# Embedding tower kernel: units in phases, four fixed slots for stacked chunks, tables and weight splitting on ACT's queue

## The reference, cut to what matters

```python
e = jnp.stack([tbl_f[ids[:, f]] for f in range(39)], axis=1)      # 2048 x 39 x 32
p, q = e[:, ROW, :], e[:, COL, :]                                 # all 741 pairs i < j
z = jnp.einsum('bpc,apc,bpa->bp', p, w, q)                        # w is 32 x 741 x 32
h = jnp.concatenate([z, dense_ctx], axis=1)                       # 757 columns
h = jnp.maximum(h @ W_top1 + b_top1, 0.0)                         # 512
h = jnp.maximum(h @ W_top2 + b_top2, 0.0)                         # 256
y = h @ W_top3                                                    # 1
```

## Time and profile before

| what | value |
|---|---|
| median of 3 runs | 873.27 us |
| the profiled execution | 877.21 us |
| its span, first to last instruction | 875.4 us |
| mean granted TensorE clock | 0.932 of full speed |
| PE busy | 734.8 us (84%) |
| DVE (VectorE) busy | 655.0 us (75%) |
| POOL (GpSimd) busy | 589.1 us (67%) |
| ACT (ScalarE) busy | 92.4 us (11%) |
| moved by DMA | 149.90 MB, mean 171 GB/s |

### The profile page before, as it was taken

One profiled execution on the slowest core, in us unless ns is written; L12 is line 12 of the kernel. 1 busy time (PEld: TensorE's weight loads), 2 busy tenths in 40 slices (PEclk: granted clock), 3 DMA queues, 4 the chain that ended last, 5 costly groups with the idle time before them and its releaser, 6 DMA issues.

```text
span 875.4 us, 11491 instructions
## 1 busy us (share of the span) xinstructions
PE 734.8 (84%) x4378; PEld 291.6 (33%) x4378; DVE 655.0 (75%) x786; ACT 92.4 (11%) x153; POOL 589.1 (67%) x752
## 2 busy tenths in 40 slices
PE   2603567387998969999999699999999799999998
PEld 1201122122332424443433244444433244444333
DVE  4603759466989947899898679999999478998750
ACT  2202000110010101010101111001111010111002
POOL 6899999998169999997599999982999940000000
PEclk9856688788999989999999899999999899999999
DMA  6677663658654567633664647444734575326000
GB/s 162 207 267 271 216 199 106 224 169 288 229 171 159 157 198 227 228 123 101 228 185 154 199 145 244 136 143 164 248 107 154 189 240 172 142 70 207 22 0 1
DMA packets 71036, 149.90 MB, mean 171 GB/s; under 512 B 12782, under 2 KB 22081, under 8 KB 70853
## 3 DMA queue, kind: packets, MB, share of 16 engines
q1 hardware_dynamic: 58684, 142.83, 47.0%
q0 software_dynamic: 12288, 6.32, 5.0%
q10 hardware_dynamic: 8, 0.01, 0.0%
HBM read 115.49 MB, written 33.62 MB: 170 GB/s over the span
## 4 chain that ended last, share of the span: by engine, by line
PE 64%; DMA 14%; DVE 12%; issue 5%; SPq 4%; ACT 1%; DVEq 0%; ACTq 0%
PE z_ps L541 21%; PE u_ps L517 20%; PE t_ps L495 8%; PE m_ps L554 7%; DVE prod L773 6%; DVE one_hot L761 5%; DMA e<-scratch 5%; DMA w_rows<-h 3%; DMA scratch<-parts 3%; PE m_ps L556 2%; DMA hot_idx<-hot 2%; PE t_ps L480 1%; SPq L412 1%; PE u_ps L576 1%; PE u_ps L585 1%
## 5 line engine op out<-in xcount | busy, mean ns | idle before, releaser
L773 DVE TENSOR_TENSOR prod<-u_ps,eT 128x1024 f32<-128x1024 f32 x400 | 469.7, 1216 | 127.6 <-PE u_ps L517 126.6
L330 POOL DMA_INDIRECT e_rows<-in_tbl_dram,idx x384 | 382.3, 996 | 121.4 <-issue 65.3
L517 PE MATMUL u_ps<-e,w 128*128 128x512 f32 x800 | 263.0, 443 | 97.0 <-DMA e<-scratch 50.6
L541 PE MATMUL z_ps<-prod,sel 128*32 128x512 f32 x1600 | 268.7, 624 | 0.0
L517 PEld LDWEIGHTS u_ps<-e,w 128*128 128x128 f32 x800 | 135.6, 195 | 244.2 <-issue 114.4
L337 POOL MEMSET pause<- 128x512 f32 x364 | 207.6, 570 | 0.2
L495 PE MATMUL t_ps<-one_hot,tb 125*32 125x512 bf16 x1560 | 150.2, 399 | 28.2 <-DVE one_hot L761 27.8
L761 DVE TENSOR_SCALAR one_hot<-hot_idx,row 125x512 bf16<-125x512 f16 (+2 forms) x320 | 155.2, 539 | 20.0 <-DMA hot_idx<-hot 16.1
L495 PEld LDWEIGHTS t_ps<-one_hot,tb 125*32 125x32 bf16 x1560 | 56.3, 101 | 124.4 <-issue 82.6
L541 PEld LDWEIGHTS z_ps<-prod,sel 128*32 128x32 f32 x1600 | 44.5, 110 | 141.4 <-issue 122.6
L554 PE MATMUL m_ps<-zT,w1s 128*128 128x512 f32 x144 | 73.2, 592 | 0.0
(11 more groups left out here) (42 smaller groups left out, 101.9 us busy)
## 6 DMA issues: line engine op xcount, KB each, us to landing
w<-w_rows SPq DMA_DIRECT2D x100, 512.0 KB, 5.4
e<-scratch SPq DMA_DIRECT2D x72, 512.0 KB, 4.9
scratch<-parts SPq DMA_DIRECT2D x72, 256.0 KB, 2.2
w_rows<-h SPq DMA_DIRECT2D x24, 512.0 KB, 6.3
e_rows<-in_tbl_dram,idx POOLq DMA_INDIRECT x384
hot_idx<-hot SPq DMA_DIRECT2D x12, 512.0 KB, 6.8
h<-in_w_dram SPq DMA_DIRECT2D x6, 512.0 KB, 4.5
e<-scratch SPq DMA_DIRECT2D x8, 384.0 KB, 4.1
```

Of the source, the lines that this page charges most:

```text
L330: pool.indirect_dma_start(e_rows[:, r, n, D * q:D * q + D], None, tables[f], bass.IndirectOffsetOnAxis(ap=idx[:, t, f * TPG + n:f * TPG + ...
L517: last = nc.tensor.matmul(u_ps[:, s % 2, place, :], w4[:, p % WR, (u % PW) * P:(u % PW + 1) * P], e4[:, chunk_no(t, g) % ES, j - C * g, :] ...
L541: last = nc.tensor.matmul(z_ps[D * quad:D * quad + D, z % 2, :], sel[:, D - 1 - row:2 * D - 1 - row], prod[:, (NS * t + n) % PR, place, :] ...
L773: nc.vector.tensor_tensor(prod[:, s % PR, :, :], u_ps[:, s % 2, :, :], e, ALU.mult).then_inc(s_mul, 1)
```

## The change

The units are ordered in phases, one for each chunk, in the order 0, 1, 2, 3, 7, 8, 4, 5, 6, 9. A phase has all units in which its chunk meets a chunk that came earlier, whichever of the two is the stacked one. The sizes of the phases are 3, 7, 11, 15, 19, 23, 27, 31, 35 and 29 units, the same as those of the ten chunks before. Chunk 7 is now needed from unit 36, chunk 8 from unit 55 (batch 13, second step), and the stacked chunk 4 from unit 86. The slices of chunks 7 and 8 are taken two to a batch, in batches 1 to 10 of a tile (in the first tile 0 to 2 and 5 to 9), and those of chunks 1 and 2 of the next tile in batches 36 to 47. `e4` has four slots and a chunk has a fixed one. `w4` has four slots instead of six. The weights are split in pieces of 16 units with two rooms, and their loads and stores and the table loads are issued by ACT. Chunk 8's tables are split in batch 1. In ACT's program, a load of weights waits until the stores of the piece two before it have landed. The copies of the ids (15 instead of 4) are one for each table. The dense layers' weights are loaded in batch 12.

```diff
+HOT_TABLES = {1: ((0, 8), (1, 10), (2, 8), (3, 8)), 2: ((1, 8), (2, 8), (3, 8)), 7: ((0, 10), (1, 8), (2, 8), (3, 8)),
+              8: ((0, 10), (1, 8), (2, 10), (3, 10))}
...
-UNITS = [(j // C, gi, j) for j in range(F) for gi in range(j // C + 1) if C * gi < j]
+PHASES = (0, 1, 2, 3, 7, 8, 4, 5, 6, 9)
+
+
+def units_of_phase(n):
+    g = PHASES[n]
+    earlier = PHASES[:n]
+    against = [(y, g, C * y + q) for y in earlier if y > g for q in range(fields_in(y))]
+    own = [(g, gi, C * g + q) for q in range(fields_in(g)) for gi in sorted(x for x in earlier if x < g) + [g] if C * gi < C * g + q]
+    return against + own
+
+
+UNITS = [u for n in range(NG) for u in units_of_phase(n)]
...
-WR = 6
-ES = 3
+WR = 4
+ES = 4
+
+E4_SLOT = {0: 0, 1: 2, 2: 3, 3: 1, 7: 2, 8: 3, 4: 0, 5: 1, 6: 0, 9: 1}
...
-PREPS = {0: (2,), 3: (3,), 11: (4,), 19: (5,), 27: (6,)}
-PREP_UNITS = [(0, 8)] + [(8 + 32 * k, 40 + 32 * k) for k in range(6)]
...
+PREP_UNITS = [(16 * k, min(NU, 16 * k + 16)) for k in range(-(-NU // 16))]
+PREPS_FIRST = 3
+PREPS = {4 * (k - PREPS_FIRST): k for k in range(PREPS_FIRST, len(PREP_UNITS))}
...
+FIRST_TILE = ((7, 0, None, (0, 0, 0, 1, 1, 1, 2, 2, 2, 2)), (3, 0, 3, ()), (8, 0, None, (5, 5, 6, 6, 7, 7, 8, 8, 9, 9)),
+              (4, 0, 14, ()), (5, 0, 21, ()), (6, 0, 28, ()), (9, 0, 35, ()),
+              (1, 1, None, (36, 37, 38, 38, 39, 39, 40, 40, 41, 41)), (0, 1, 42, ()), (2, 1, 43, (43, 44, 45, 45, 46, 46, 47, 47)))
+OTHER_TILES = ((3, 0, 0, ()), (7, 0, None, (1, 1, 2, 2, 3, 3, 4, 4, 5, 5)), (8, 0, None, (6, 6, 7, 7, 8, 8, 9, 9, 10, 10)),
+               (4, 0, 14, ()), (5, 0, 20, ()), (6, 0, 27, ()), (9, 0, 35, ()),
+               (1, 1, None, (36, 37, 38, 38, 39, 39, 40, 40, 41, 41)), (0, 1, 42, ()), (2, 1, 43, (43, 44, 45, 45, 46, 46, 47, 47)))
+LAST_TABLE_BATCH = 1
```

SP's list ahead of the first batch becomes:

```diff
             sp.wait_ge(s_hot16, 32)
             load_hot_indices((0, 1))
             load_hot_indices((0, 2))
...
             bring_piece(0, 0)
+            bring_piece(0, 1)
+            load_hot_indices((0, 7))
             store_parts((0, 1))
-            stack_chunk((0, 1))
-            store_weights(1)
-            load_weights(2)
             store_parts((0, 0))
             stack_chunk((0, 0))
-            for p in range(1, 5):
-                bring_piece(0, p)
-            load_table(8)
+            stack_chunk((0, 1))
             store_parts((0, 2))
+            bring_piece(0, 2)
             stack_chunk((0, 2))
```

ACT's program gets the loads and stores:

```diff
+            def load_weights(k):
+                a, b = PREP_UNITS[k]
+                if k >= 2:
+                    act.wait_ge(s_wout[k % 2], 64 * (k // 2))
+                act.dma_start(w_in_room[k % 2][:, 0:(b - a) * D], w[:, a * P:b * P].rearrange("a (s n) -> a s n", s=C)
+                              ).then_inc(s_wraw[k % 2], 16)
...
+            def weights_rest(k):
+                a, b = PREP_UNITS[k]
+                act.wait_ge(s_wlo, k + 1)
+                for h in range(2):
+                    act.dma_start(w_rows[:, h, 1, a * P:b * P].rearrange("a (s n) -> a s n", s=C),
+                                  w_in_room[k % 2][:, 0:(b - a) * D]).then_inc(s_wout[k % 2], 16)
+                if k + 2 < len(PREP_UNITS):
+                    load_weights(k + 2)
...
+            load_table(1)
+            load_weights(0)
+            load_weights(1)
             act.wait_ge(s_idx, 16)
...
+            load_table(2)
             act.wait_ge(s_idt, 1)
...
             table_high(1)
+            weights_high(0)
             table_middle(1)
-            weights_high(0)
             table_high(2)
+            weights_rest(0)
+            load_table(7)
             table_middle(2)
+            weights_high(1)
+            table_high(7)
+            weights_rest(1)
+            table_middle(7)
             take_chunk((0, 1))
-            weights_high(1)
             take_chunk((0, 0))
-            table_high(7)
-            table_middle(7)
+            weights_high(2)
             take_chunk((0, 2))
-            table_high(8)
-            table_middle(8)
+            load_table(8)
+            weights_rest(2)
             for t in range(NT):
                 for b in range(NBAT):
                     if t == 0 and b in PREPS:
-                        for k in PREPS[b]:
-                            weights_high(k)
+                        weights_high(PREPS[b])
+                        weights_rest(PREPS[b])
+                    if t == 0 and b == LAST_TABLE_BATCH:
+                        table_high(HOT_CHUNKS[-1])
+                        table_middle(HOT_CHUNKS[-1])
```

VectorE's list ahead of the first batch:

```diff
             table_rest(1)
+            weights_low(0)
             table_low(1)
+            table_rest(2)
...
-            for k in range(slices_of(1)):
+            for k in range(OS):
                 one_hot_slice((0, 1), k)
-            weights_low(0)
-            table_rest(2)
             table_low(2)
+            weights_low(1)
+            table_rest(7)
+            for k in range(OS, slices_of(1)):
+                one_hot_slice((0, 1), k)
+            table_low(7)
             split_chunk((0, 1))
-            weights_low(1)
...
             split_chunk((0, 0))
+            weights_low(2)
...
-            table_rest(7)
-            table_low(7)
             split_chunk((0, 2))
-            table_rest(8)
-            table_low(8)
+            for c, k in TAKES.get(0, ()):
+                one_hot_slice(c, k)
```

More of the change, by code:

```diff
@@ L132, in rows_count, with e4_before, e4_loads @@
     n = GPOS[c]
-    return sum(16 * TPG * gathered(GATHERED[x][1]) for x in range(n % ER, n + 1, ER))
+    return sum(16 * TPG * len(gathered(GATHERED[x])) for x in range(n % ER, n + 1, ER))
+def e4_before(c):
+    t, g = c
+    same = [x for x in PHASES if E4_SLOT[x] == E4_SLOT[g]]
+    n = same.index(g)
+    return (t, same[n - 1]) if n else (t - 1, same[-1]) if t else None
+def e4_loads(c):
+    same = [x for x in PHASES if E4_SLOT[x] == E4_SLOT[c[1]]]
+    return len(same) * c[0] + same.index(c[1]) + 1
 TURNS, TAKES, COMPLETE, INDICES, STACKS = {}, {}, {}, {}, {}
@@ L166, in spread_mlp @@
         slices = sum(list(x[3]).count(b) for x in OTHER_TILES if not (last and x[1]))
-        work[b] = 3 * slices + (2 if any(x[2] == b for x in OTHER_TILES) else 0)
+        work[b] = 3 * slices + (3 if any(x[2] == b for x in OTHER_TILES) else 0)
     taken = []
@@ L238, in tower @@
         hroom = h1[:, :, :].rearrange("p m n -> p (m n)")
-        w_in_room = hroom[:, 0:2 * NB]
-        w_hi_room = hroom[:, 2 * NB:4 * NB].bitcast(F32R)
+        w_in_room = [hroom[:, k * NB:(k + 1) * NB] for k in range(2)]
+        w_hi_room = [hroom[:, (2 + k) * NB:(3 + k) * NB].bitcast(F32R) for k in range(2)]
         ids_f = prod[:, 0, :, :].rearrange("p u n -> p (u n)")[:, 0:NT * HOT_FIELD_COLS]
         def table_room(g):
-            first, rows = HOT_ROWS[g, 0], sum(HOT_SLICES[g][1])
+            first, rows = HOT_ROWS[g, 0], sum(HOT_SLICES[g])
             if g == HOT_CHUNKS[-1]:
@@ L326, in _ @@
                     pool.wait_ge(s_tp, GPOS[c] - ER + 1)
-                for q in range(gathered(g)):
+                for q in gathered(c):
                     f = C * g + q
@@ L595, in _ @@
             transpose_ids()
-            for g, turned, slices in BEGIN:
-                if turned:
+            for g in BEGIN:
+                if gathered((0, g)):
                     turn((0, g))
-                for k in slices:
-                    look_up((0, g), k)
+                if hot((0, g)):
+                    for k in range(slices_of(g)):
+                        look_up((0, g), k)
             pe.wait_ge(s_sel, 16)
@@ L753, in one_hot_slice @@
                 for tall in (False, True):
[L754 removed]
+                    here = [(i, x) for i, x in enumerate(fields) if (HOT_SLICES[g][x] > HK) == tall]
                     for a, (i, x) in enumerate(here):
```

171 lines of the change are left out of this document (76 added, 95 removed), and 3 rows, old and new, of the table OTHER_TILES.

## The result

The changed kernel takes 871.6 us (median of 20 runs, 866.98 to 875.05) against 874.46 us for the kernel before (20 runs, 872.66 to 878.73). The ratio is 0.9965, 95% interval 0.995 to 0.9979: faster by a third of a per cent, where 848 was forecast and 868 was the end of the range. The profiled execution took 875.05 us, the slowest of the 20; its span is 872.9 us, against 875.4.

The account below looks back on a forecast made before the run. It took the start and tile 0 (301 us, waits in queue order) and then DVE or PE by batch as bounds. 877.2 - 39 + 14 = 852, as a median 848; own range 834 to 862, 8 in 10 822 to 868.

Parts of the forecast that it names:

- The start: Before the first multiply: it comes at 59 us instead of 75.3, -16 us; 54 to 65 with other store landings.
- the price of a 256 KB store: In the start, ACT waits for weight stores to land: 4.5 us taken, between 3.2 and 6.3.
- its own first sign of being wrong: Wrong if the start is late because ACT's waits for stores are longer than 4.5 us.
- Tile 0: First tile: DVE's work of 176 us plus waits, 203 taken; it ends at 262 instead of 301.1, -23 for the tile.
- Chunk 3 was to be 7 us late: Tile 0: chunk 3, turned in batch 3 behind chunk 7's slices and wanted in batch 5, comes 7 us late.
- Tiles 1 to 3: Later tiles: 190, 190 and 181 us instead of 185.4, 183.7 and 178.6, +14 us in all.
- The wait in batch 2: Tiles 1 to 3: PE's wait for stacked chunk 2 goes, -8.6, -9.6 and -9.2 us at most.
- the wait in batch 13: Tiles 1 to 3: a new wait for stacked chunk 8, 4 us idle and 1 for the clock.
- (d): Rival: ACT is tile 0's bottleneck, standing for stores; tile 0 gains nothing, only the start does: 871 us, chance 0.08.
- (b): Rival: transfers, not waiting, bound the start; the first multiply stays near 75 us: 864 us, chance 0.14.
- (a): Rival: the new wait for chunk 8 does not come; tiles 1 to 3 at 185: 833 us, chance 0.17.
- (c): Rival: chunks 7 and 8 come late in every tile, 19 us a tile instead of 5: 899 us, chance 0.09.

Follow-up runs that it names:

- third_first: Changed kernel with the edits of late_load and early_slices, plus the first tile's chunk 3 turned in batch 0 ahead of chunk 7's slices: 833.85 us, ratio 0.9536.
- late_load: Changed kernel with ACT loading a weight piece after rounding the one before, not right behind the stores it must wait for: 854.4 us, ratio 0.9768.
- early_slices: Changed kernel with the slices of chunks 7 and 8 one batch earlier in tiles 1 to 3: 860.67 us, ratio 0.9847.
- short one-hots: Changed kernel and kernel before, one-hots of chunks 7 and 8 in tiles 1 to 3 cut to 32 columns: 858.88 and 871.87 us beside 876.31.
- queues_only: Changed kernel with the order of units, batches of turns and slices, ES = 3 and WR = 6 of before: 863.37 us, ratio 0.9873.
- four_slots: Kernel before with four slots for stacked chunks and the next tile's first chunks taken earlier: 877.29 us beside 902.24, ratio 0.9716.

## Why the prediction was wrong, step by step

**The start: wrong, and 16.9 us of the miss.** The failing step is the price of a 256 KB store: "between 3.2 and 6.3 us I take 4.5". The median is 3.6, but the one pair on which ACT stood took 15.9 from the first issue (58.0) to the landing (73.9), outside both ends; each store by itself took 8.3 and 11.6 from its own issue. The chain of the prediction gives the pair 5.5 us (51.5 to 57), so that this term alone is 10.4 us short. Both ends were medians over the whole span, while this store leaves when two stacks, a table of four DMAs and the scratch stores are all under way, and a third stack comes at 67. The prediction gave the share of the earlier trace rows as 0.78 and used it only for a rival; it should have bounded the landing by it. A second term was too small: ACT took chunks 1, 0 and 2 at 44, 46 and 55 instead of 37, 39 and 47, since DVE's last seven slices of chunk 1 took 9 us, not 6, and began 3 later. By that the stores left at 58.0 instead of 51.5, the other 6.5 us. The prediction had named the first of these as its own first sign of being wrong. With the late load the first multiply came at 59.3, but that it is the number forecast is luck: there ACT takes chunk 2 at 50, not 47, and waits for no store ahead of the first multiply.

**Tile 0: right in sum (207.6 for 203), not in its terms.** Chunk 3 was to be 7 us late; PE waited 15.1 us for it, and the batch took 12 too many:

```profile
120.84 1.65 PE L518 MATMUL u_ps<-e,w 128*128 128x512 f32 x3 [15.13 <-DMA e<-scratch]
```

DVE's wait for chunk 8's tables was there, 2.3 and 1.3 us for the 4 forecast. `third_first` shows the wait for chunk 3 to be order alone. With one term twice its size, the nearness of the sum is in part luck.

**Tiles 1 to 3: right.** 189.9, 190.5 and 182.7 for 190, 190 and 181. The wait in batch 2 went, batches 0 to 9 cost what DVE costs (48.3 for 46), and the wait in batch 13 came (3.8, 4.6 and 2.2 for 5, in tile 1 half of it idle and the rest nearly all the clock). PE was busier beside DVE than the 70% foreseen (41.0 of 48.3 us). `early_slices` shows that wait, and the short one-hots show the mix of work.

**The rivals.** (d) gave 871, the nearest in number, but by luck: it has the start gain 16 us and tile 0 nothing, and the trace has it the other way round. It named the mechanism, ACT standing for its stores, and put it after the first multiply instead of ahead of it. (b) gave 864 with the first multiply near 75, where it was, and its engines were full. But `late_load` moves the first multiply to 59 with engines at 0.99, so transfers did not set it. The stores were slow, in part by the tables ahead of them and for the rest, as argued, by the full engines; a wait in ACT's program made that matter. The Trainium skill, DMA: Bandwidth & Descriptors, section Issuing engines are not separate DMA queues, says that issuing from several engines saves only issue time; `queues_only` agrees in so far as the move to ACT left the first multiply at 74.0 against 75.3, and no run shows that rule as the cause. (a) did not come. (c) came for one chunk of two, at 2.2 to 4.6 us a tile instead of 19.

**The chances.** The start hung on a store's landing and on when ACT takes its chunks, and the range gave 54 to 65 us for the first alone. With a landing of 16 us, the prediction's own chain ends at 69.4; with the late takes it ends at 75.9, and the whole at 865. So the upper end of 868 left 3 us for all else, and tile 0 and tiles 1 to 3 took 6.7.

## What to carry to other kernels

A wait that comes right behind its own transfer in an engine's program costs the landing time at that moment, not the median: put the wait where the thing it guards is needed, behind other work of that engine. When a queue's work is moved to an engine that computes, count what stands behind each wait there. When work of one engine is moved from batches in which another engine is full to batches in which it is alone, it stops being free; look for the resource that forced the order (here a slot) before reordering.

## What the runs showed of the hardware that was not expected

A DMA issue is not of fixed cost. ACT's issues of stores took 0.53 us at least and 0.63 in the median, and up to 4.25 us at 58.0, where the engines were 0.92 to 0.97 busy and ACT executed nothing else. The view of the tensor that they write, in the changed kernel (issue min/median/max in ns, first and last start; then times to landing of all transfers of this tensor):

```profile
L664 ACTq DMA_DIRECT2D w_rows<-h x26: 525/625/4251, 14.4 to 231.8; - x26
...
DMA to landing us min/median/max: 2.2/3.5/11.6
```

In batch 13 an idle of TensorE of 1.9 us (tile 1) and one of 2.8 (tile 2) were each followed by half the clock for 3.4 us, while one of 2.0 us in the same batch of tile 3 was not:

```profile
724.35 0.50 PE L518 MATMUL u_ps<-e,w 128*128 128x512 f32 x1 [1.98 <-DMA e<-scratch]
724.69 1.88 PE L555 MATMUL m_ps<-zT,w1s 128*128 128x512 f32 x4
```

And chips differ: on one of them the kernel before took 902 us. It was not profiled there, but `four_slots` was. Its first multiply came at 100.3 us, where the kernel before has it at 75.3 on another chip, while its tiles 1 to 3 took what four slots lead one to expect. DVE idles 20.8 us of that start in two waits between one-hots of chunk 1. The profile does not name what released them. It is not the indices, for which the program waits only ahead of the first of these one-hots; the cause stays open.
